# Attention stage of a four-layer block: q computed by tokens, its squares summed by POOL and DVE, its copy turned by PE

## What is computed

```python
q = (hidden_states @ Wq).reshape(B, Sq, H, D)          # H = 16 heads, D = 128
k = (encoder_hidden_states @ Wk).reshape(B, Skv, H, D)
v = (encoder_hidden_states @ Wv).reshape(B, Skv, H, D)
q = rmsnorm(q, gq)                # x * rsqrt(mean(x*x, -1) + eps) * g
k = rmsnorm(k, gk)
scores = einsum("bqhd,bkhd->bhqk", q, k) * scale
attn = softmax(scores)
x = x + einsum("bhqk,bkhd->bqhd", attn, v).reshape(B, Sq, H * D) @ Wo
```

## Time and profile before

| | us |
|---|---|
| median of 3 runs | 2483.26 (2483.11 to 2485.51) |
| the profiled execution | 2479.53 |
| its span, first to last instruction | 2477.7 |

### The profile page before, as it was taken

How to read it: one execution, slowest core, us unless ns; L and a number is a source line. 1 busy time by engine, 2 the same in 40 slices (tenths; PEclk the granted TensorE clock), 3 DMA queues, 4 the chain that set the end, 5 groups by cost and what they waited for, 6 DMA issues and landing times. The chain is left out here.

```text
span 2477.7 us, 31987 instructions
## 1 busy us (share of the span) xinstructions
PE 2260.7 (91%) x10784; PEld 1745.7 (70%) x10784; DVE 1768.8 (71%) x3390; ACT 1291.6 (52%) x2246; POOL 1366.2 (55%) x1107
## 2 busy tenths in 40 slices
PE   5899999999999999999695899899899986999994
PEld 4788888888888888888551666566566554777773
DVE  7676776777677676766585898898898996634344
ACT  3555555554555555555475766766766653223331
POOL 2444444444444444444185887997998993233331
PEclk9999999999999999999897999999999997899997
DMA  7655555464645545452446766565565532369865
GB/s 298 239 192 197 183 183 200 154 217 170 218 161 194 193 172 206 158 204 107 161 139 232 250 190 208 166 209 180 174 206 176 188 107 89 120 225 347 335 216 194
DMA packets 148066, 480.77 MB, mean 194 GB/s; under 512 B 24577, under 2 KB 61697, under 8 KB 124481
## 3 DMA queue, kind: packets, MB, share of 16 engines
q1 hardware_dynamic: 138208, 449.78, 51.7%
q0 software_dynamic: 7520, 24.74, 2.8%
q10 hardware_dynamic: 2176, 4.19, 0.4%
HBM read 361.19 MB, written 117.47 MB: 193 GB/s over the span
## 5 line engine op out<-in xcount | busy, mean ns | idle before, releaser
L671 POOL TENSOR_SCALAR att_probs<-att_probs,att_recip 128x512 f32<-128x512 f32 x256 | 179.2, 703 | 377.3 <-DVE att_recip L765 377.3
L1918 POOL TENSOR_TENSOR mix_drive<-mix_du,mix_rows 128x512 f32<-128x512 f32 x256 | 326.5, 1282 | 36.8 <-DMA mix_rows<-bc_d 9.4
L1989 DVE TENSOR_TENSOR_SCAN mix_state<-mix_state,mix_drive 128x512 f32<-128x512 f32 x256 | 312.9, 1222 | 42.4 <-POOL mix_drive L1918 30.1
L563 ACT ACTIVATE att_probs<-att_s,att_bias,att_rq 128x512 f32<-128x512 f32 x256 | 199.9, 781 | 226.9 <-DVE att_bias L761 226.6
L1772 ACT ACTIVATE mix_state<-mix_delta,mix_a 128x512 f32<-128x512 f32 x256 | 175.9, 690 | 217.8 <-DVE mix_drive L2000 188.0
L1903 POOL TENSOR_TENSOR mix_y<-mix_y,mix_drive 128x512 f32<-128x512 f32 x180 | 230.7, 1282 | 46.5 <-DVE mix_drive L2000 46.3
L1682 PE MATMUL mix_down<-mix_wd,mix_hT 128*128 128x512 f32 x512 | 233.9, 600 | 7.7 <-DVE residual_x L2020 7.7
L569 ACT CAST att_pT<-att_pt 128x512 fp32r<-128x512 f32 x256 | 143.6, 591 | 174.1 <-PE att_pt L385 169.5
L760 DVE TENSOR_REDUCE att_nmax<-att_s 128x1 f32<-128x512 f32 x256 | 174.8, 683 | 62.8 <-PE att_s L101 62.7
L801 DVE TENSOR_TENSOR att_pT<-att_pt,att_pT 128x512 fp32r<-128x512 f32 x256 | 170.1, 685 | 65.0 <-ACT att_pT L569 58.3
L1682 PEld LDWEIGHTS mix_down<-mix_wd,mix_hT 128*128 128x128 f32 x512 | 98.1, 192 | 110.1 <-issue 96.1
(11 more groups left out here) (384 smaller groups left out, 6670.8 us busy)
## 6 DMA issues: line engine op xcount, KB each, us to landing
mix_gu<-guT SPq DMA_DIRECT2D x64, 1024.0 KB, 8.3
att_xn<-normT SPq DMA_DIRECT2D x31, 2048.0 KB, 8.6
split_w<-att_expert_w SPq DMA_DIRECT2D x32, 1536.0 KB, 6.4
lead_w<-split_w SPq DMA_DIRECT2D x16, 3072.0 KB, 12.1
mix_rows<-bc_d SPq DMA_DIRECT2D x128, 256.0 KB, 5.0
att_cx<-ctxT SPq DMA_DIRECT2D x30, 1024.0 KB, 8.6
guT<-att_ffnT SPq DMA_DIRECT2D x32, 512.0 KB, 6.1
mix_wd<-wdT SPq DMA_DIRECT2D x16, 1024.0 KB, 7.9
```

Of the source, the lines that this page charges most:

```text
L563: act.activation(probs[:, n, :], ps_s[n % 2][:, :], ACT.Exp, bias=bias[:, n:n + 1], scale=rq[:, n:n + 1], accum_out=sums[:, n:n + 1]).then ...
L671: pool.tensor_scalar(probs[:, n, :], probs[:, n, :], recip[:, n:n + 1], 1.0, ALU.mult, ALU.mult).then_inc(s_pn, 1)
L1918: pool.tensor_tensor(drive[q % RING][:, :], du[i % DUS][:, :], rows[g % ROWS][:, 0, :], ALU.mult).then_inc(s_drive, 1)
L1989: dve.tensor_tensor_scan(h[:, :], h[:, :], drive[q % RING][:, :], 0.0, ALU.mult, ALU.add).then_inc(s_scan, 1)
```

## The change

- PE makes q with tokens in the partitions: `queries(half, bank)`, 24 products of 256 columns a half, into the same two banks.
- ACT copies each half to SBUF (`copy_q`, new tile `att_qn`). It makes no squares.
- POOL squares the copy in one instruction of 128x1024 (`square_q`) into `att_ksq`, the tile of k's squares, and DVE sums it (`sum_q`, a reduction and a small scaling). `square_q` stands between `norm_p(i, 7)` and `split_ffn`.
- PE turns the copy, head by head (`turn_q`, four turns each), back into banks 2 and 0; ACT and DVE take the high and low halves from there (`q_hi`, `q_lo`), later than before.
- `sums_q`, the tile of squares `att_qsq` and the column of ones are gone.

```diff
-                def queries(h, bank):
-                    d = slice(h * D, (h + 1) * D)
-                    for k in range(KD):
-                        mm = split_product(pe, ps_w[bank][:, :], (wpart(0, "q", k)[:, d], wpart(1, "q", k)[:, d]),
-                                           (xn[:, 0, k, :], xn[:, 1, k, :]), k == 0, k == KD - 1)
+                def queries(half, bank):
+                    for a in range(2):
+                        t = 2 * half + a
+                        rows = slice(t * P, (t + 1) * P)
+                        for k in range(KD):
+                            mm = split_product(pe, ps_w[bank][:, a * W2:(a + 1) * W2],
+                                               (xn[:, 0, k, rows], xn[:, 1, k, rows]),
+                                               (wpart(0, "q", k), wpart(1, "q", k)), k == 0, k == KD - 1)
                     mm.then_inc(s_q, 1)
+
+                def turn_q(j, h, bank):
+                    pe.wait_ge(s_qc, 2 * j + 2)
+                    for t in range(TB):
+                        tr = pe.transpose(ps_w[bank][:, t * P:(t + 1) * P], qn[:, t, h, :], ident_sb[:, :])
+                    tr.then_inc(s_qt, 1)
-                def sums_q():
-                    for n in range(HP * TB):
-                        h, t = divmod(n, TB)
-                        mm = pe.matmul(ps_o[:, n:n + 1], qsq[:, h, t * P:(t + 1) * P], ones[:, :], start=True, stop=True)
-                    mm.then_inc(s_ss, 1)
...
-                def q_parts(j, h):
-                    bank = ps_w[(2, 0)[h]]
-                    act.wait_ge(s_q, 2 * j + h + 1)
-                    act.copy(qT[:, 0, h, :], bank[:, :]).then_inc(s_qhi, 1)
-                    act.activation(qsq[:, h, :], bank[:, :], ACT.Square).then_inc(s_qsq, 1)
+                def copy_q(j, half):
+                    act.wait_ge(s_q, 2 * j + half + 1)
+                    act.copy(qn[:, 2 * half:2 * half + 2, :, :], ps_w[(2, 0)[half]][:, :]).then_inc(s_qc, 1)
+
+                def q_hi(j, h):
+                    act.wait_ge(s_qt, 2 * j + h + 1)
+                    act.copy(qT[:, 0, h, :], ps_w[(2, 0)[h]][:, :]).then_inc(s_qhi, 1)
...
+                def square_q(j):
+                    pool.wait_ge(s_qc, 2 * j + 2)
+                    pool.wait_ge(s_kss, j + 1)
+                    pool.tensor_tensor(ksq[:, :, :, :], qn[:, :, :, :], qn[:, :, :, :], ALU.mult).then_inc(s_qsq, 1)
...
-                def sum_q(j):
-                    dve.wait_ge(s_ss, j + 1)
-                    dve.tensor_scalar(qss[:, :], ps_o[:, 0:TB * HP], 1.0 / D, RMS_EPS, ALU.mult, ALU.add).then_inc(s_qss, 1)
+                def sum_q(own, j):
+                    dve.wait_ge(s_qsq, j + 1)
+                    own.after(dve.tensor_reduce(qss[:, :], ksq[:, :, :, :].rearrange("p t h d -> p h t d"), AX_X, ALU.add))
+                    dve.tensor_scalar(qss[:, :], qss[:, :], 1.0 / D, RMS_EPS, ALU.mult, ALU.add).then_inc(s_qss, 1)
```

More of the change, by code:

```diff
@@ L198, in stage_attention @@
         s_kt, s_kthi, s_ktlo = m.sem("kT"), m.sem("kT_hi"), m.sem("kT_lo")
-        s_q, s_qhi, s_qsq, s_qlo = m.sem("q"), m.sem("q_hi"), m.sem("q_squared"), m.sem("q_lo")
+        s_q, s_qc, s_qsq = m.sem("q"), m.sem("q_copied"), m.sem("q_squared")
+        s_qt, s_qhi, s_qlo = m.sem("qT"), m.sem("q_hi"), m.sem("q_lo")
         s_kss, s_rk, s_qss = m.sem("k_sums"), m.sem("rk"), m.sem("q_squares")
-        s_ss, s_rq, s_power = m.sem("q_sums"), m.sem("rq"), m.sem("power_done")
+        s_rq, s_power = m.sem("rq"), m.sem("power_done")
         s_v, s_vhi, s_vlo = m.sem("v"), m.sem("v_hi"), m.sem("v_lo")
@@ L447, in _ @@
                 turn_k(0, 1)
+                turn_q(0, 0, 2)
+                turn_q(0, 1, 0)
                 pe.wait_ge(s_qlo, 1)
                 turn_k(1, 2)
[L450 to L452 removed]
                 pe.wait_ge(s_qlo, 2)
@@ L505, in iteration @@
                         turn_k(0, 1)
-                        pe.wait_ge(s_qlo, 2 * j + 1)
-                        turn_k(1, 2)
+                        turn_q(j, 0, 2)
                     turn_p(i, b, 1, 0)
@@ L510, in iteration @@
                     if not last:
+                        turn_q(j, 1, 0)
+                        pe.wait_ge(s_qlo, 2 * j + 1)
+                        turn_k(1, 2)
+                    turn_p(i, b, 1, 2)
+                    if not last:
                         pe.wait_ge(s_qlo, 2 * j + 2)
                         kv(cx, "v", 0, 0, s_v)
[L513 to L517, removed]
                     turn_p(i, b, 1, 3)
@@ L604, in _ @@
                 norm_hi(1)
-                q_parts(0, 0)
-                q_parts(0, 1)
+                copy_q(0, 0)
+                copy_q(0, 1)
                 norm_hi(2)
@@ L610, in _ @@
                 kt_hi(0, 0)
+                q_hi(0, 0)
+                q_hi(0, 1)
                 kt_hi(0, 1)
@@ L638, in iteration @@
                     if not last:
-                        q_parts(j, 0)
+                        copy_q(j, 0)
                     exp(i, 7)
                     if not last:
-                        q_parts(j, 1)
+                        copy_q(j, 1)
                     ffn_out(i, b)
@@ L648, in iteration @@
                         kt_hi(j, 0)
+                        q_hi(j, 0)
+                    pt_hi(i, b, 1, 0)
+                    pt_hi(i, b, 1, 1)
+                    if not last:
+                        q_hi(j, 1)
                         kt_hi(j, 1)
-                    for k in range(TB):
-                        pt_hi(i, b, 1, k)
+                    pt_hi(i, b, 1, 2)
+                    pt_hi(i, b, 1, 3)
                     expert_hi(i)
@@ L718, in _ @@
                 norm_k(0)
+                square_q(0)
                 invert(3)
@@ L734, in iteration @@
                     norm_p(i, 7)
+                    if not last:
+                        square_q(j)
                     split_ffn(i)
@@ L867, in _ @@
                 scale_k(0)
-                q_lo(0, 0)
-                q_lo(0, 1)
                 norm_stats(3)
@@ L874, in _ @@
                 kt_lo(0, 0)
+                q_lo(0, 0)
+                q_lo(0, 1)
                 kt_lo(0, 1)
-                sum_q(0)
+                sum_q(own, 0)
                 normalize(3)
@@ L908, in iteration @@
                     pt_lo(i, b, 0, 3)
-                    if not last:
-                        q_lo(j, 0)
                     row_recip(i, 7)
@@ L913, in iteration @@
                         scale_k(j)
-                        q_lo(j, 1)
                     if i == 0:
@@ L920, in iteration @@
                         kt_lo(j, 0)
-                        kt_lo(j, 1)
+                        q_lo(j, 0)
                     pt_lo(i, b, 1, 0)
                     pt_lo(i, b, 1, 1)
+                    if not last:
+                        q_lo(j, 1)
+                        kt_lo(j, 1)
+                        sum_q(own, j)
                     pt_lo(i, b, 1, 2)
-                    if not last:
-                        sum_q(j)
                     pt_lo(i, b, 1, 3)
```

12 lines of the change are left out of this document (6 added, 6 removed).

## The result

| | before | with the change |
|---|---|---|
| median of 4 runs, us | 2483.35 (2483.11 to 2485.51) | **2554.07** (2553.30 to 2558.99) |
| the profiled execution, us | 2479.53 | 2558.99 |
| its span, us | 2477.7 | 2556.2 |

The ratio is 1.0287, 95% interval 1.0272 to 1.0301: the change costs 70.7 us. 2556 was forecast.

A forecast was written before the change was run, and what follows sets the result against it. PE was taken to bound the kernel (busy 35.16 of 35.39 us an iteration). Waits +85 (31 x 2.75), clock -15, falls brought back +2: +72 on the profiled 2479.5, 2552; median 3.7 higher, 2556; range 2488 to 2578.

## What to carry to other kernels

An instruction given to an idle engine is not free if it holds another engine's critical instructions, as POOL's square holds DVE's scaling here: place it where the other engine has nothing of that kind to do, or hand the critical work to an engine that isn't held (54 and 56 us here, with no work saved). Where it can't be moved, cut it into pieces, because the victim got one instruction through at each change (39 us here). And moving an operand's finished form later, as q's halves here, starts a chain through three engines whose whole length must fit under PE's remaining work: turning q half a `pv` earlier, with its halves, the order of the turns and the sum moved along, was worth 42 us together (2499.7 to 2458.0). Against the kernel before, PE's shorter program is worth 15.

## What the runs showed of the hardware that I had not expected

- The hold is paid for each waiting instruction, not once. Eight scalings that need 1.66 us took 2.35 beside short POOL instructions, 3.92 beside a square in four pieces, 5.06 beside one square and 6.51 beside two.
- It costs POOL next to nothing: the last `norm_p`, which starts while a scaling runs, takes 0.77, and the one before it in the same iteration 0.69.
- A fall of the clock has no fixed price. It was 1.25 us in the kernel before; in the changed one it is 0.1 to 1.0 in whole iterations and 1.6 in iteration 31. What goes with it changed from one-column products to standing still, while the count stayed nearly the same (12 and 13). Had I only counted the falls, I would have said that the turns changed nothing.
